# An eight-layer recurrent block with routed experts: the row of ones from the relu, the last norms reordered, 18 constant products in the head

## The chip, the cores and the metric

The kernel runs on one core of one Trainium2 chip, in one launch. The metric is the device time in microseconds of one execution; lower is better. Three executions of the kernel before gave 852.19 us in the median (851.09 to 852.88).

## The reference

The input x has 8 sequences of 512 rows of 128. It is normalised once (xn), and two branches read xn:

- Eight layers of linear attention and a feed-forward part: k and q go through elu + 1, `kv` is the sum over the sequence of k times v, `att = q kv z`, then `h = LN(h + att Wo + bo)` and `h = LN(h + gelu(h W1 + c1) W2 + c2)`, and a last norm. 
- One routed expert per sequence: the mean over the sequence of a normalised xn, a softmax over 8 experts, the largest taken, and with that expert's weights

```python
h = jax.nn.relu(jnp.einsum('bsd,bdh->bsh', z, W_down[idx]) + b_down[idx][:, None, :])
y = jnp.einsum('bsh,bhd->bsd', h, W_up[idx]) + b_up[idx][:, None, :]
return y * gate[:, None, None]
```

The output is `x + s * silu(expert branch)`, with s the first branch.

## The kernel before, in words

A unit is one sequence in one layer: 64 units. Work is staged as a software pipeline over 66 periods, each of about 12.7 us; in period p the attention of unit p, the first norm of unit p - 1, the feed-forward of unit p - 2 and the second norm of unit p - 3 run on the engines beside the projection of k and q for unit p + 1 and the transposes of the state of unit p + 2. The order on each engine is written by hand: `pe_period`, `act_period`, `dve_period` and `pool_period` give one period's instructions for TensorE, ScalarE, VectorE and GpSimd, and semaphores tie them together. Products are in f32; the k, q and up projections are split into a high and a low part (three products each), and an f32 product of TensorE leaves two records in the profile.

**The head.** SyncE and ScalarE issue the first loads. GpSimd makes the constants (ident, mean_f32, ones, centre, and later a memset of the last partition of `e_hid`, 1x4096, L1448), each counted in `const_ready`; it also forms the residual rows and the first `res_att` (L1051, L1054). VectorE takes statistics (L372, L376) and normalises the first two sequences. TensorE folds the first layer's weights (`pe_fold_att_first`, L238 and L241), transposes the first state (`pe_state_transpose`, L668), projects k and q (`pe_kq`, L680 to L682), turns the vector rows (`pe_cols`), and makes the first state product (`pe_kz`, L690). In period 0 VectorE copies g_sb (L1125), lays out the layers' vectors (`dve_cols`) and in `dve_affines` copies 4 columns (L194) and forms two matrices (L196, L198), before the shift of the third sequence and `dve_q_ks` (L1144); statistics of two more sequences follow in the same period.

**The experts.** After the routing in the last layer SyncE loads each sequence's expert: W_down (128x64), b_down, W_up with b_up as a 65th row. `pe_expert_down` (L592) multiplies into 64 partitions, `act_expert_relu` (L597) writes 64 partitions of `e_hid`, whose 65th partition holds the ones that GpSimd's memset wrote, and `pe_expert_up` (L610) contracts over 65 partitions, so that the row of ones brings in b_up.

**The last layer.** A finished sequence w gets a second norm and then the final one. In the periods 61 and 62 ScalarE normalises z_tm (`act_norm2`, L920) and directly behind it the final norm of sequences 0 and 1 (`act_final_norm`, L928), both at the period's end, ahead of the next period's gelu. `dve_den`/`dve_rden` (L1158) are in every period. Behind the last period the order is written out: TensorE does up, down, the transposes of z1 (L727) and expert products; VectorE does `dve_h2_tail` (L1205), statistics of seven slots (`dve_tail_stats`, L1241, L1245; they fill `tl_mv`), `dve_tail_shift` (L1249, L1251) and for sequences 6 and 7 `dve_last_affine` (gain step L1213, scale step L1218) in PSUM; ScalarE does the last rstd's (`act_tail_rstd`, L941, L943), and the silus (L630) after one more table load; GpSimd multiplies and adds (L1284, L1289) and the sequences go out.

Of the kernel before, what the change touches and what calls it, by code (L numbers as in the profile page):

```python
# [6 lines left out]
P = 128  # L7
# [4 lines left out]
def build(nc, x, Wq, bq, Wk, bk, Wv, bv, Wo, bo, g1, be1, g2, be2, W1, c1, W2, c2, gf, bef,  # L12
# [23 lines left out]
    with ExitStack() as ctx:  # L36
# [197 lines left out]

        def pe_fold_att_first(pe):
            pe.wait_ge(s["const_ready"], CONSTS_EARLY)
            pe.wait_ge(s["raw_a0"], 3 * 16)
            nc.tensor.matmul(up_ps[1][:, 0:3 * D], centre[:, :], raw_att[:, :, :].rearrange("p a d -> p (a d)"),  # L238
                             start=True, stop=False)
            pe.wait_ge(s["raw_b0"], 3 * 16)  # L240
            nc.tensor.matmul(up_ps[1][:, 0:3 * D], mean_f32[0:1, :], b_row[0:1, 0:3 * D],  # L241
                             start=False, stop=True).then_inc(s["xa_ps"], 1)
# [80 lines left out]
        ew_down = sb("ew_down", [P, SEQS, HID])  # L323
        eb_down = sb("eb_down", [HID, SEQS])
# [33 lines left out]
        CONSTS, CONSTS_EARLY = 12, 6  # L358
# [213 lines left out]
        def pe_expert_down(pe, i):  # L572
# [19 lines left out]
            nc.tensor.matmul(e_down_bank[i][0:HID, :], ew_down[:, w, :], zf_fm[:, w, :], start=True, stop=True).then_inc(s["e_down"], 1)  # L592

        def act_expert_relu(act, i):
            w = EXPERTS[i]
            act.wait_ge(s["e_down"], i + 1)
            nc.scalar.activation(e_hid[0:HID, i, :], e_down_bank[i][0:HID, :], ACT.Relu,  # L597
                                 bias=eb_down[:, w:w + 1]).then_inc(s["e_hid_s"], 1)

        def pe_expert_up(pe, i):  # L600
            w = EXPERTS[i]
            pe.wait_ge(s["e_hid_s"], i + 1)
            if i == 0:
                pe.wait_ge(s["const_ready"], CONSTS)
            elif i == 1:
                pe.wait_ge(s["h1_s"], UNITS)
# [318 lines left out]
        def act_final_norm(act, w):  # L925
            for t in range(TT):
# [32 lines left out]
        def act_period(act, l, b, between=None, behind_keys=None):  # L959
# [15 lines left out]
            if proj:  # L975
                act_q_exp(act, p + 1)
            if p == UNITS - 1:
                act_expert_relu(act, 0)
                act_norm2(act, p, (b - 3) % SEQS)
# [10 lines left out]
            if fin and p < UNITS - 1:  # L990
                act_final_norm(act, p - 5 - FIRST_LAST)
# [216 lines left out]
        def dve_last_affine(dve, w, slot):  # L1208
            bank = tail_ps[w]
            dve.wait_ge(s["tl_mv_s"], TT * (slot + 1))  # L1210
            for t in range(TT):
                i = slot * TT + t
                nc.vector.scalar_tensor_tensor(bank[:, t, :], bank[:, t, :], tl_mv[:, i, 0:1], fin_bc[:, 0, :],  # L1213
                                               ALU.subtract, ALU.mult).then_inc(s["last_c"], 1)
            dve.wait_ge(s["last_c"], TT * (w - 5))
# [31 lines left out]
        def dve_tail_shift(dve, first, last, calls):  # L1247
# [3 lines left out]
            nc.vector.tensor_scalar(tl_sh[:, c], tl_m[:, c], -1.0, 1.0, ALU.mult, ALU.add).then_inc(s["tl_sh_s"], 1)  # L1251
# [109 lines left out]
        with nc.Block() as block:  # L1361
            @block.sync
            def _(sp):
# [40 lines left out]
                for b in range(SEQS):  # L1404
                    e = sp.value_load(expert_i[b:b + 1, 0:1], min_val=0, max_val=E - 1)
                    sp.dma_start(ew_down[:, b, :], W_down[bass.ds(e, 1)].rearrange("a d h -> d (a h)")).then_inc(expert_in[b], 16)
                    sp.dma_start(eb_down[:, b:b + 1], b_down[bass.ds(e, 1)].rearrange("a h -> h a")).then_inc(expert_in[b], 16)
# [9 lines left out]
            def _(pool):  # L1417
# [30 lines left out]
                nc.gpsimd.memset(e_hid[HID:HID + 1, :, :], 1.0).then_inc(c, 1)  # L1448
                pool.wait_ge(c, 11)
                nc.gpsimd.iota(expert_m8[:, :], pattern=[[1, E]], base=-E, channel_multiplier=0,  # L1450
# [26 lines left out]
            def _(pe):  # L1477
                pe_fold_att_first(pe)
                pe_state_transpose(pe, 0, 0)
                pe.wait_ge(s["qk_ready"], 2)  # L1480
                pe_period(pe, -1, SEQS - 1)
                pe_cols(pe)
                pe_period(pe, 0, 0, lambda: pe_fold_w1_first(pe))
# [11 lines left out]
                pe_down(pe, last - 1, range(TT))  # L1495
                pe_z1_transpose(pe, last, UNITS)
                pe_expert_up(pe, 1)
# [69 lines left out]
            def _(dve):  # L1567
# [58 lines left out]
                dve_expert_gate(dve, 1)  # L1626
                dve_h2_tail(dve, last)
# [5 lines left out]
                dve_last_affine(dve, 6, S_W6)  # L1633
                dve.wait_ge(s["tl_r_s"], 2)
                dve_tail_shift(dve, S_F5, S_F5, 2)
                dve_last_affine(dve, 7, S_W7)
# [33 lines left out]
```

## Time and profile before

| what | value |
|---|---|
| median of three executions | 852.19 us (851.09 to 852.88) |
| the profiled execution's own time | 852.55 us |
| its span | 850.8 us |
| TensorE busy | 806.7 us, 95% of the span |
| VectorE busy | 764.9 us, 90% |
| ScalarE busy | 735.8 us, 86% |
| GpSimd busy | 415.2 us, 49% |

The profile is of one execution. A row of the timeline gives start, duration, engine, line and operation, and in brackets how long the engine was idle before it and what ended that. Transposes and matmuls of one group stand in one row with xN records. A busy TensorE is not TensorE at its peak: its records overlap, and their length depends on the granted clock.

### The profile page before, as it was taken

Reading aid. Unit: us, or ns where it says so; the run is one execution under the profiler, and the core shown is the slowest. Engines: PE = TensorE matmul, PEld = TensorE weight load, DVE = VectorE, ACT = ScalarE, POOL = GpSimd, SP = SyncE. Lnnn points to the kernel's source line nnn. Section 1 sums busy time; section 2 is a strip of 40 time slices with the busy share of each in tenths; the row PEclk is TensorE's granted clock in tenths of the full one; section 3 lists DMA queues with packets and bytes.
Section 4 is the critical chain, followed back from the end, with each engine's and each line's share of the span. In section 5 each row is a group of like instructions: output and inputs, shape, how many; then the busy total and the mean of one; then the engine's idle time right before and its main releaser. Section 6 shows DMA issues by size and latency. Waiting matters only on the chain.

```text
span 850.8 us, 19233 instructions
## 1 busy us (share of the span) xinstructions
PE 806.7 (95%) x5914; PEld 734.9 (86%) x5914; DVE 764.9 (90%) x2670; ACT 735.8 (86%) x1315; POOL 415.2 (49%) x395
## 2 busy tenths in 40 slices
PE   5698999999999999999999999999999999999993
PEld 3588899989999999999999999999999998988862
DVE  5888998999999898999899898998999898999877
ACT  2479999988999899988999899998999899989875
POOL 5243444454544454544454444444454454456667
PEclk9789999999999999999999999999999999999996
DMA  5300200101010100101010000101000000000002
GB/s 149 90 2 1 45 1 2 35 2 44 2 35 2 45 2 1 35 2 45 1 27 11 25 20 2 35 2 45 1 21 16 1 2 2 1 20 8 1 14 87
DMA packets 26264, 18.76 MB, mean 22 GB/s; under 512 B 4354, under 2 KB 22195, under 8 KB 26164
## 3 DMA queue, kind: packets, MB, share of 16 engines
q1 hardware_dynamic: 25300, 16.95, 7.2%
q8 instruction: 49, 0.80, 0.4%
q10 hardware_dynamic: 864, 0.59, 0.2%
q14 instruction: 51, 0.42, 0.2%
HBM read 15.43 MB, written 2.10 MB: 21 GB/s over the span
## 4 chain that ended last, share of the span: by engine, by line
PE 80%; DVE 9%; ACT 6%; issue 3%; POOL 1%; DMA 0%; POOLq 0%; ACTq 0%; DVEq 0%
PE down_ps L759 21%; PE att_ps L720 7%; PE small_ps L690 6%; PE up_ps L749 5%; PE up_ps L751 5%; PE up_ps L750 5%; PE t_ps L668 5%; PE t_ps L727 4%; PE kq_ps L680 3%; PE kq_ps L681 3%; PE kq_ps L682 3%; DVE z_lo L1044 3%; ACT z_hi L914 2%; PE up_ps L711 2%; PE small_ps L698 2%
## 5 line engine op out<-in xcount | busy, mean ns | idle before, releaser
L759 PE MATMUL down_ps<-w_use,hid 128*128 128x128 f32 x2048 | 259.5, 275 | 0.7 <-ACT hid L865 0.7
L759 PEld LDWEIGHTS down_ps<-w_use,hid 128*128 128x128 f32 x2048 | 243.8, 192 | 2.7 <-ACT hid L865 2.7
L1062 POOL TENSOR_TENSOR res_ffn<-z_tm,g_ffn 128x512 f32<-128x512 f32 x64 | 81.9, 1279 | 241.2 <-DVE k_e L1175 235.9
L1051 POOL TENSOR_TENSOR res_att<-z_tm,g_att 128x512 f32<-128x512 f32 x64 | 82.5, 1288 | 155.1 <-DVE h L1002 155.1
L865 ACT ACTIVATE hid<-up_ps 128x512 f32<-128x512 f32 x192 | 113.4, 592 | 22.2 <-PE up_ps L751 14.7
L1014 DVE BATCH_NORM_STATS2 st<-h 128x6 f32<-128x128 f32 x504 | 107.5, 276 | 0.1
L920 ACT ACTIVATE z_tm<-h,shift,rstd 128x128 f32<-128x128 f32 x248 | 101.5, 482 | 1.3 <-DVE shift L1031 1.3
L749 PE MATMUL up_ps<-z_hi,w_hi 128*128 128x512 f32 x192 | 86.4, 450 | 2.2 <-ACT hid L865 1.7
L1065 POOL TENSOR_TENSOR res_ffn<-res_ffn,ffn_row 128x512 f32<-128x512 f32 x64 | 84.0, 1313 | 5.0
L1054 POOL TENSOR_TENSOR res_att<-res_att,att_row 128x512 f32<-128x512 f32 x64 | 82.3, 1286 | 5.0
L680 PE MATMUL kq_ps<-w_kq_hi,zq_hi 128*128 128x256 f32 x256 | 82.0, 320 | 1.5 <-DVE zq_lo L957 1.5
L985 ACT ACT_TABLE_LOAD x63 | 80.8, 1283 | 1.1
L966 ACT ACT_TABLE_LOAD x62 | 79.5, 1283 | 1.1
L751 PE MATMUL up_ps<-z_lo,w_hi 128*128 128x512 f32 x192 | 75.6, 394 | 0.0
L750 PE MATMUL up_ps<-z_hi,w_lo 128*128 128x512 f32 x192 | 75.3, 392 | 0.0
L690 PEld LDWEIGHTS small_ps<-k_phi,z_tm 128*128 128x128 f32 x512 | 68.1, 194 | 7.5 <-DVE k_phi L1182 2.1
L1039 DVE TENSOR_SCALAR z_tm<-h,rstd,shift 128x128 f32<-128x128 f32 x256 | 71.5, 343 | 2.3
L681 PE MATMUL kq_ps<-w_kq_lo,zq_hi 128*128 128x256 f32 x256 | 73.2, 286 | 0.0
L682 PE MATMUL kq_ps<-w_kq_hi,zq_lo 128*128 128x256 f32 x256 | 72.8, 285 | 0.0
L1044 DVE TENSOR_TENSOR z_lo<-t_ps,z_hi 128x512 fp32r<-128x512 f32 x64 | 44.3, 692 | 31.6 <-ACT z_hi L914 31.6
L690 PE MATMUL small_ps<-k_phi,z_tm 128*128 128x128 f32 x512 | 68.6, 277 | 2.0 <-DVE k_phi L1182 2.0
L720 PE MATMUL att_ps<-kvo,q_n 128*128 128x128 f32 x512 | 69.6, 280 | 0.0
(223 smaller groups left out, 1966.4 us busy)
## 6 DMA issues: line engine op xcount, KB each, us to landing
raw_w<-in_L_attn_W SPq DMA_DIRECT2D x15, 256.0 KB, 4.6
out_y<-gate_tm SPq DMA_DIRECT2D x8, 256.0 KB, 2.2
bias_bc<-in_L_attn_c SPq DMA_DIRECT2D x7, 256.0 KB, 4.8
x_tm<-in_L_attn_x SPq DMA_DIRECT2D x3, 512.0 KB, 7.8
raw_rows<-in_L_attn_be SPq DMA_DIRECT2D x15, 64.0 KB, 4.3
raw_g<-in_L_attn_g SPq DMA_DIRECT2D x14, 64.0 KB, 3.2
x_tm<-in_L_attn_x SPq DMA_DIRECT2D x2, 256.0 KB, 3.5
raw_rows<-in_L_attn_bo SPq DMA_DIRECT2D x8, 64.0 KB, 3.9
```

The costliest lines, as they stand in the source:

```text
L680: nc.tensor.matmul(to, tile(zq_hi, t), w_kq_hi[:, :], start=True, stop=False)
L681: nc.tensor.matmul(to, tile(zq_hi, t), w_kq_lo[:, :], start=False, stop=False)
L682: last = nc.tensor.matmul(to, tile(zq_lo, t), w_kq_hi[:, :], start=False, stop=True)
L690: last = nc.tensor.matmul(G_PS, z_tm[:, b, t, :], k_phi[:, t, :], start=(t == 0), stop=(t == TT - 1))
L720: last = nc.tensor.matmul(att_ps[:, t, :], tile(q_n, t), kvo[:, :], start=True, stop=True)
L749: nc.tensor.matmul(up_bank[j], w_hi, z1_hi[:, :], start=True, stop=False)
L750: nc.tensor.matmul(up_bank[j], w_lo, z1_hi[:, :], start=False, stop=False)
L751: nc.tensor.matmul(up_bank[j], w_hi, z1_lo[:, :], start=False, stop=True).then_inc(s["up"], 1)
L759: last = nc.tensor.matmul(down_ps[:, t, :], hid[:, j, t * P:(t + 1) * P], w2_use[:, j, :], start=(j == 0), stop=(j == FC - 1))
L865: nc.scalar.activation(hid[:, j, :], up_bank[j], ACT.Gelu).then_inc(s["gelu"], 1)
L920: nc.scalar.activation(z_tm[:, b, t, :], h2[:, b % 2, t, :], ACT.Identity, scale=rstd[:, i:i + 1], bias=shift[:, i:i + 1]).then_inc(s["z2n ...
L1014: nc.vector.bn_stats(st[:, first + t, :], h[:, t, :]).then_inc(s[st_s], 1)
```

## The change

Seven edits, in the order of the diff:

1. `pe_keep_busy` issues products of two constants, ident and centre, into `att_ps`, which nothing has used yet: 8 ahead of the fold of the first weights, 4 behind the transposes of the first state, 6 behind `pe_cols`.
2. `ew_down` gets a 65th column of zeros for each sequence and `eb_down` a 65th partition of ones, both by small memsets on GpSimd, in place of the memset of `e_hid`; the product goes into 65 partitions and the relu of 0 + 1 writes the ones. `const_ready` counts one more, and the wait for it moves from `pe_expert_up(0)` to `pe_expert_down(0)` and the first relu.
3. `act_final_norm` is called for two tiles behind q_exp, and for two at the period's end.
4. `dve_last_affine` becomes `dve_last_gain` and `dve_last_scale`, and the gain steps stand earlier in VectorE's order.
5. `tl_sh` is computed by a subtraction of two tensors instead of a tensor_scalar.
6. For the last unit but one the last tile of down stands behind the transposes of z1.
7. The two loads into the enlarged tiles write the first 64 columns and partitions.

```diff
@@ -232,8 +232,14 @@
+        def pe_keep_busy(pe, products):
+            for _ in range(products):
+                nc.tensor.matmul(att_ps[:, 0, :], ident[:, :], centre[:, :], start=True, stop=True)
         def pe_fold_att_first(pe):
             pe.wait_ge(s["const_ready"], CONSTS_EARLY)
+            pe_keep_busy(pe, 8)
             pe.wait_ge(s["raw_a0"], 3 * 16)
             nc.tensor.matmul(up_ps[1][:, 0:3 * D], centre[:, :], raw_att[:, :, :].rearrange("p a d -> p (a d)"),
                              start=True, stop=False)
@@ -320,8 +326,9 @@
         wr_sb = sb("wr_sb", [P, E])
         br_bc = sb("br_bc", [SEQS, E])
         expert_i = sb("expert_i", [SEQS, 1], I32)
-        ew_down = sb("ew_down", [P, SEQS, HID])
-        eb_down = sb("eb_down", [HID, SEQS])
+        ew_down = sb("ew_down", [P, SEQS, HID + 1])
+        eb_down = sb("eb_down", [HID + 1, SEQS])
         ew_up = sb("ew_up", [HID + 1, SEQS, D])
         e_hid = sb("e_hid", [HID + 1, SEQS, S])
         st_x = sb("st_x", [P, SEQS * TT, 6])
@@ -355,7 +362,7 @@
         tl_r = sb("tl_r", [P, 7 * TT])
         tl_m = sb("tl_m", [P, 7 * TT])
         tl_sh = sb("tl_sh", [P, 7 * TT])
-        CONSTS, CONSTS_EARLY = 12, 6
+        CONSTS, CONSTS_EARLY = 13, 6
@@ -589,20 +596,22 @@
                 pe.wait_ge(s["z1lo_s"], UNITS)
             elif i == 7:
                 pe.wait_ge(s["gelu"], (UNITS - 1) * FC + 3)
-            nc.tensor.matmul(e_down_bank[i][0:HID, :], ew_down[:, w, :], zf_fm[:, w, :], start=True, stop=True).then_inc(s["e_down"], 1)
+            if i == 0:
+                pe.wait_ge(s["const_ready"], CONSTS)
+            nc.tensor.matmul(e_down_bank[i][0:HID + 1, :], ew_down[:, w, :], zf_fm[:, w, :], start=True, stop=True).then_inc(s["e_down"], 1)
         def act_expert_relu(act, i):
             w = EXPERTS[i]
             act.wait_ge(s["e_down"], i + 1)
-            nc.scalar.activation(e_hid[0:HID, i, :], e_down_bank[i][0:HID, :], ACT.Relu,
+            if i == 0:
+                act.wait_ge(s["const_ready"], CONSTS)
+            nc.scalar.activation(e_hid[:, i, :], e_down_bank[i][0:HID + 1, :], ACT.Relu,
                                  bias=eb_down[:, w:w + 1]).then_inc(s["e_hid_s"], 1)
         def pe_expert_up(pe, i):
             w = EXPERTS[i]
             pe.wait_ge(s["e_hid_s"], i + 1)
-            if i == 0:
-                pe.wait_ge(s["const_ready"], CONSTS)
-            elif i == 1:
+            if i == 1:
                 pe.wait_ge(s["h1_s"], UNITS)
             if i < TANH:
                 pe.wait_ge(s["ew_scaled"], i + 1)
@@ -922,8 +931,9 @@
-        def act_final_norm(act, w):
-            for t in range(TT):
+        def act_final_norm(act, p, w, tiles):
+            act.wait_ge(s["shift_s"], p)
+            for t in tiles:
                 i = 2 * TT + t
                 nc.scalar.activation(z_tm[:, w, t, :], z_tm[:, w, t, :], ACT.Identity, scale=rstd[:, i:i + 1],
                                      bias=shift[:, i:i + 1]).then_inc(s["zf_n"], 1)
@@ -974,6 +984,8 @@
                 behind_keys()
             if proj:
                 act_q_exp(act, p + 1)
+            if fin and p < UNITS - 1:
+                act_final_norm(act, p, p - 5 - FIRST_LAST, (0, 1))
             if p == UNITS - 1:
                 act_expert_relu(act, 0)
                 act_norm2(act, p, (b - 3) % SEQS)
@@ -988,7 +1000,7 @@
             if ln2 and p < UNITS - 1:
                 act_norm2(act, p, (b - 3) % SEQS)
             if fin and p < UNITS - 1:
-                act_final_norm(act, p - 5 - FIRST_LAST)
+                act_final_norm(act, p, p - 5 - FIRST_LAST, (2, 3))
             if between:
                 between()
@@ -1205,13 +1217,16 @@
             nc.vector.tensor_tensor(tail_ps[u - FIRST_LAST][:, :, :], down_ps[:, :, :], res_ffn[:, u % 2, :, :],
                                     ALU.add).then_inc(s["h2_s"], 1)
-        def dve_last_affine(dve, w, slot):
+        def dve_last_gain(dve, w, slot):
             bank = tail_ps[w]
             dve.wait_ge(s["tl_mv_s"], TT * (slot + 1))
             for t in range(TT):
                 i = slot * TT + t
                 nc.vector.scalar_tensor_tensor(bank[:, t, :], bank[:, t, :], tl_mv[:, i, 0:1], fin_bc[:, 0, :],
                                                ALU.subtract, ALU.mult).then_inc(s["last_c"], 1)
+        def dve_last_scale(dve, w, slot):
+            bank = tail_ps[w]
             dve.wait_ge(s["last_c"], TT * (w - 5))
             for t in range(TT):
                 i = slot * TT + t
@@ -1248,7 +1263,7 @@
             c = slice(first * TT, last * TT + TT)
             nc.vector.tensor_tensor(tl_m[:, c], tl_mv[:, c, 0], tl_r[:, c], ALU.mult).then_inc(s["tl_mr_s"], 1)
             dve.wait_ge(s["tl_mr_s"], calls)
-            nc.vector.tensor_scalar(tl_sh[:, c], tl_m[:, c], -1.0, 1.0, ALU.mult, ALU.add).then_inc(s["tl_sh_s"], 1)
+            nc.vector.tensor_tensor(tl_sh[:, c], ones[:, c], tl_m[:, c], ALU.subtract).then_inc(s["tl_sh_s"], 1)
         def dve_final_norm(dve, w):
             dve.wait_ge(s["shift_s"], UNITS - 1)
@@ -1403,8 +1418,8 @@
                 sp.wait_ge(s["routed"], 1)
                 for b in range(SEQS):
                     e = sp.value_load(expert_i[b:b + 1, 0:1], min_val=0, max_val=E - 1)
-                    sp.dma_start(ew_down[:, b, :], W_down[bass.ds(e, 1)].rearrange("a d h -> d (a h)")).then_inc(expert_in[b], 16)
-                    sp.dma_start(eb_down[:, b:b + 1], b_down[bass.ds(e, 1)].rearrange("a h -> h a")).then_inc(expert_in[b], 16)
+                    sp.dma_start(ew_down[:, b, 0:HID], W_down[bass.ds(e, 1)].rearrange("a d h -> d (a h)")).then_inc(expert_in[b], 16)
+                    sp.dma_start(eb_down[0:HID, b:b + 1], b_down[bass.ds(e, 1)].rearrange("a h -> h a")).then_inc(expert_in[b], 16)
                     sp.dma_start(ew_up[0:HID, b, :], W_up[bass.ds(e, 1)].rearrange("a h d -> h (a d)")).then_inc(expert_in[b], 16)
                     sp.dma_start(ew_up[HID:HID + 1, b, :], b_up[bass.ds(e, 1)]).then_inc(expert_in[b], 16)
@@ -1445,8 +1460,10 @@
                 pool_w2(pool, 0, False)
                 pool_period(pool, 0, 1)
                 pool.wait_ge(s["t2m"], 2)
-                nc.gpsimd.memset(e_hid[HID:HID + 1, :, :], 1.0).then_inc(c, 1)
+                nc.gpsimd.memset(eb_down[HID:HID + 1, :], 1.0).then_inc(c, 1)
                 pool.wait_ge(c, 11)
+                nc.gpsimd.memset(ew_down[:, :, HID:HID + 1], 0.0).then_inc(c, 1)
+                pool.wait_ge(c, 12)
                 nc.gpsimd.iota(expert_m8[:, :], pattern=[[1, E]], base=-E, channel_multiplier=0,
                                allow_small_or_imprecise_dtypes=True).then_inc(c, 1)
                 pool.wait_ge(c, CONSTS)
@@ -1477,9 +1494,11 @@
             def _(pe):
                 pe_fold_att_first(pe)
                 pe_state_transpose(pe, 0, 0)
+                pe_keep_busy(pe, 4)
                 pe.wait_ge(s["qk_ready"], 2)
                 pe_period(pe, -1, SEQS - 1)
                 pe_cols(pe)
+                pe_keep_busy(pe, 6)
                 pe_period(pe, 0, 0, lambda: pe_fold_w1_first(pe))
                 for b in range(1, SEQS):
                     pe_period(pe, 0, b)
@@ -1492,8 +1511,9 @@
                 last = UNITS - 1
                 pe_up(pe, last - 1, UNITS, range(FC))
                 pe_expert_down(pe, 1)
-                pe_down(pe, last - 1, range(TT))
+                pe_down(pe, last - 1, (0, 1, 2))
                 pe_z1_transpose(pe, last, UNITS)
+                pe_down(pe, last - 1, (3,))
                 pe_expert_up(pe, 1)
                 pe_up(pe, last, UNITS, range(FC))
                 pe_down(pe, last, range(TT))
@@ -1624,16 +1644,18 @@
                 dve_tail_stats(dve, S_F4, z_tm[:, 4], s["y_s"], 5)
                 dve_tail_stats(dve, S_W6, small_ps, s["h2_s"], p - 1)
                 dve_expert_gate(dve, 1)
+                dve_last_gain(dve, 6, S_W6)
                 dve_h2_tail(dve, last)
                 dve.wait_ge(s["tl_r_s"], 1)
                 dve_tail_shift(dve, S_F3, S_F4, 1)
                 dve_tail_stats(dve, S_W7, down_ps, s["h2_s"], p)
                 dve_tail_stats(dve, S_F5, z_tm[:, 5], s["y_s"], 6)
-                dve_last_affine(dve, 6, S_W6)
+                dve_last_scale(dve, 6, S_W6)
+                dve_last_gain(dve, 7, S_W7)
                 dve.wait_ge(s["tl_r_s"], 2)
                 dve_tail_shift(dve, S_F5, S_F5, 2)
-                dve_last_affine(dve, 7, S_W7)
+                dve_last_scale(dve, 7, S_W7)
                 dve_tail_stats(dve, S_F6, small_ps, s["y_d"], TT)
                 dve_tail_stats(dve, S_F7, down_ps, s["y_d"], 2 * TT)
```

## Rows read from the trace of the kernel before

**Rows 1.** The page: span, and the chain that ended last, by engine.

```profile
span 850.8 us, 19233 instructions
...
PE 80%; DVE 9%; ACT 6%; issue 3%; POOL 1%; DMA 0%; POOLq 0%; ACTq 0%; DVEq 0%
```

**Rows 2.** The chain of work from 0 to 60 us: start, us, what.

```profile
20.36 3.25 DVE lv L194
```

**Rows 3.** Timeline, GpSimd and VectorE, 18 to 24 us: start, us, engine, line, op.

```profile
18.73 1.26 POOL L1054 TENSOR_TENSOR res_att<-res_att,att_row 128x512 f32<-128x512 f32 x1
...
19.68 0.29 DVE L1125 COPY g_sb<-small_ps 128x128 f32<-128x128 f32 x1 [0.97 <-PE small_ps L690]
...
20.06 3.50 POOL L1448 MEMSET e_hid<- 1x4096 f32 x1
...
23.63 0.34 DVE L196 TENSOR_SCALAR aff_att<-centre,lv 128x128 f32<-128x128 f32 x1
```

**Rows 4.** All executions of line L194, durations in ns.

```profile
L194 DVE TENSOR_SCALAR lv<-layer_vecs x8: 152/154/3236, 20.4 to 657.7; 128x4 f32<-128x4 f32 x8
```

**Rows 5.** Timeline of the head: GpSimd's centre, then TensorE's products.

```profile
1.94 0.45 POOL L1427 TENSOR_TENSOR centre<-ident,mean_f 128x128 f32<-128x128 f32 x1
...
5.87 1.62 PE L238 MATMUL up_ps<-raw_att,centre 128*128 128x384 f32 x2 [5.87 <-DMA raw_att<-in_L_attn_Wv]
...
8.99 1.11 PE L668 MATMUL t_ps<-ident,z_tm 128*128 128x128 f32 x4
...
12.17 0.41 PE L682 MATMUL kq_ps<-w_kq_hi,zq_lo 128*128 128x256 f32 x1
...
12.38 0.41 PE L680 MATMUL kq_ps<-w_kq_hi,zq_hi 128*128 128x256 f32 x1
...
17.57 2.07 PE L690 MATMUL small_ps<-k_phi,z_tm 128*128 128x128 f32 x8 [1.97 <-DVE k_phi L1182]
...
23.45 0.28 PE L682 MATMUL kq_ps<-w_kq_hi,zq_lo 128*128 128x256 f32 x1
```

**Rows 6.** Tile x_tm from 5.7 to 6.2 us: its loads' landing; then VectorE's timeline.

```profile
DMA to landing us min/median/max: 6.9/7.4/7.8
...
13.21 0.86 DVE L372 BATCH_NORM_STATS2 st_x<-x_tm 128x6 f32<-128x128 f32 x4
```

**Rows 7.** Timeline of periods 62 and 63, by engine.

```profile
791.15 0.60 ACT L914 ACTIVATE z_hi<-t_ps 128x512 fp32r<-128x512 f32 x1 [0.98 <-PE t_ps L727]
...
795.22 1.64 ACT L928 ACTIVATE z_tm<-z_tm,shift,rstd 128x128 f32<-128x128 f32 x4
...
797.39 0.50 PE L749 MATMUL up_ps<-z_hi,w_hi 128*128 128x512 f32 x1 [0.86 <-ACT hid L865]
...
800.57 1.27 POOL L1268 TENSOR_TENSOR z_tm<-z_tm,fin_bc 128x512 f32<-128x512 f32 x1
...
800.76 1.13 DVE L1158 TENSOR_SCALAR den_e<-den 128x64 f32<-128x64 f32 x1
```

**Rows 8.** Timeline of the tail, 816 to 840 us, by engine.

```profile
816.53 0.50 PE L749 MATMUL up_ps<-z_hi,w_hi 128*128 128x512 f32 x1 [0.52 <-DVE z_lo L1044]
...
824.10 0.70 DVE L1205 TENSOR_TENSOR down_ps<-down_ps,res_ffn 128x512 f32<-128x512 f32 x1 [2.72 <-PE down_ps L759]
...
824.93 1.19 DVE L1251 TENSOR_SCALAR tl_sh<-tl_m 128x8 f32<-128x8 f32 x1
...
828.64 1.10 DVE L1213 SCALAR_TENSOR_TENSOR small_ps<-small_ps,tl_mv,fin_bc 128x128 f32<-128x128 f32 x4
...
830.82 0.43 DVE L1249 TENSOR_TENSOR tl_m<-tl_mv,tl_r 128x4 f32<-128x4 f32 x1
...
836.57 0.30 ACT L941 ACTIVATE tl_ln<-tl_mv,eps_col 128x8 f32<-128x8 f32 x1 [1.34 <-DVE tl_mv L1245]
...
839.19 1.27 POOL L1284 TENSOR_TENSOR gate_tm<-gate_tm,z_tm 128x512 f32<-128x512 f32 x1 [1.48 <-ACT gate_tm L630]
```

**Rows 9.** Windows: us, busy time of each engine (records), granted clock (PEclk), DMA.

```profile
29.60:33.50 3.90, 3.87 (x17) 3.63 (x18) 2.49 (x5) 1.59 (x4) 0.00 (x0) 0.50 0.37 71
```

## The prediction

> **What bounds the kernel now.** I read the page first. TensorE carries 80% of the chain that ended last [rows 1]. So in the 60-odd middle periods, whose code the change leaves alone, nothing is to be had. The change touches the first 25 us, where TensorE waits for data and for small VectorE steps, and the last 75 us, where the expert part and the norms hang on VectorE and ScalarE. I therefore read the chain at the start. One step there is out of scale: VectorE's L194, 3.25 us for a copy of 4 numbers per partition [rows 2]. The timeline of the two engines around it shows why: GpSimd's memset of e_hid runs from 20.06 for 3.50, to 23.56, L194 starts inside it, and its successor L196 starts at 23.63 [rows 3]. The same line takes 0.154 us in the median of its 8 executions [rows 4]. VectorE was held until GpSimd let go.
>
> **Part 1, the row of ones out of the relu.** Taken away: one memset of 1x4096 on GpSimd, 3.50 us. Added: a memset of 1x8, one of 128x8 with a wait more, one column in each of 8 expert weights and one partition in each of 8 relus; the moving 512 columns of a product stay 512. No row shows memsets of that form: the bounds are nothing, and 0.3 us for both on VectorE's path if they hold it as the long one did; I take 0.15. What L194 gives back is 3.25 - 0.15 = 3.1 us [rows 2, 4], all of it on the path: L196, L198, the shift of x and the first q_ks L1144 stand behind it on VectorE. That is the gain if nothing else moved.
>
> **Part 2, the 18 products.** Two records each, 36 records on TensorE. The matmuls of the head run at the low level, 1.2 GHz: a record of kq takes 0.41 us at 12.17 and the next starts 0.21 later; at 23.45, the last of its kind before the first q_ks, it takes 0.28 [rows 5]. (The column of the granted clock shows no low value so early; I go by the durations.) L690's eight records of 128 columns f32 take 2.07 with their tail, so about 0.21 to 0.24 each at the low level, and I take 0.21, the step of kq's, and half of it at the high level. 16 records are 3.4 us. The first eight products start when centre is there, near 2.4, and end near 5.8; L238 starts at 5.87, when its weights have landed [rows 5]. They cost nothing, but with no margin: up to 0.2 us if they start late. The next four (8 records, 1.7 us low, 0.9 high) stand between the transposes, which end at 10.1, and L680 at 11.61, which waits for VectorE's zq_lo; cost 0 to 0.2. The last six (12 records, 2.6 low, 1.4 high) begin near 15.6 and must be through when k_phi is, 17.57: at the low level they are 0.6 us late, at the high level not at all.
>
> What they can give: TensorE would be continuously busy from 2.4 on instead of from 5.87. In the kernel before its records became short only at 23.45, after it had worked through kv and kq(1); 4 us of work from 5.87 to 10.1, a third of it with a single row of weights, did not do it [rows 5]. With 7 us on end I take the high level as reached before kq(0), with 4 chances in 5. Then kq(0), 12 records at 0.21 us, saves 1.2 to 1.4 us, the transposes and L690 1.0 more [rows 5]. Little of that arrives. First, stats of the third sequence need x_tm, issued at 5.74 with 6.9 us to landing, so 12.6, against 13.21 now: VectorE's aggregate ends at most 0.6 earlier, and ScalarE's rstd stands before q_exp in its order [rows 6]. So k_phi gains about 1.6 us, and g_sb, 19.68 now, comes near 17.3. Second, and this decides, GpSimd's pair on res_att holds VectorE then: its second half L1054 runs 18.73 to 19.99 [rows 3], its start is set by GpSimd's own order and by landings that the change leaves alone. L194 and the two L196, L198 behind it are of the kind that was held. I expect L196 at about 20.05 instead of 23.63: 3.6 us for parts 1 and 2 together, less the 0.15 for the small memsets, so **3.4 us**, 0.3 more than part 1 alone. Behind it VectorE is busy without a gap up to q_nt, so this arrives.
>
> The Trainium skill, TensorE: Matmul & The Clock Gate, What's actually happening, says the array's default is the throttled clock and activity releases it. By that rule all of kq(0), L690 and kq(1) run at 2.4 GHz, and by their rows the clock alone would be worth some 3.6 us; the trace agrees as far as 23.45, where records got short after work. What it leaves to the end is the business of rival D.
>
> **Part 3, act_final_norm in two halves (periods 61 and 62).** ScalarE idles 0.98 us before z1_hi L914 at 791.15; two of the four tiles of L928 (half of 1.64) fit in. What is left before gelu is 0.8 us shorter, and TensorE's idle before L749 at 797.39, 0.86 us, which ScalarE's hid ends, closes by that much [rows 7]. Twice, so at most 1.6. VectorE takes part back: den_e L1158 at 800.76 is held for 1.13 us by GpSimd's L1268 of 800.57 [rows 7], and where VectorE arrives earlier it meets GpSimd's operation before that. Bounds 0 and 1.6; I take **1.0**.
>
> **Part 4, z1 transposes before the last tile of down.** They free z1_hi and z1_lo earlier by up to a tile of down. TensorE then has that tile and expert_up(1) to do before it can start up; the gain can't exceed the 0.52 us that it idles before L749 at 816.53 [rows 8]. Bounds 0 and 0.52; **0.3**.
>
> **Part 5, last_affine split.** VectorE idles 2.72 us before L1205 at 824.10; the gain step of sequence 6 (L1213, 1.10 us at 828.64) goes in there. What then ends earlier is tl_mv of the last slot, for which ScalarE's L941 waits (836.57, idle 1.34), then the table load, the first silu and GpSimd's L1284 at 839.19, idle 1.48 [rows 8]. All three idle times exceed 1.1. **1.1**. The gain step of sequence 7 only swaps with a wait that is over by then: 0.
>
> **Part 6, tl_sh by tensor_tensor.** tl_sh L1251 takes 1.19 us at 824.93, held by GpSimd. But tl_m L1249, a tensor_tensor out of SBUF, takes 0.43 us at 830.82 as well [rows 8]: this form is held too. So 0; bounds: a gain of 1.0 if it were not, a loss of 1.2 if the second shift, which now slips through, is caught.
>
> By the Trainium skill, SBUF — State Buffer, SBUF: two separate sides, a VectorE operation with two SBUF inputs is locked out by a GpSimd operation that reads SBUF. The trace agrees, with the 0.43 us; this speaks against part 6.
>
> **The sum.** 3.4 + 1.0 + 0.3 + 1.1 = 5.8 us off the profiled execution, whose own time was 852.55 (span 850.8 [rows 1] and 1.75 around it). The median shown, 852.19, lies 0.36 lower; I subtract from it: **846.4 us**.
>
> **Rivals.** (B) The clock stays low through the head. The last six products then delay L690 by 0.6, and part 1 gives 3.1 - 0.6 = 2.5: total 4.9, 847.3. For it: 4 us of work near 6 us did not lift the clock. 0.15. (C) The tail gives back: VectorE, arriving earlier, is caught by one more GpSimd operation (1.26 us each) at the second tl_sh or at den_e. Part 5 or 3 is lost, total about 3.9: 848.3. For it: L1158 and L1251 are both caught now. 0.18. (D) VectorE's L194 and L196 slip between GpSimd's two halves. Then the 2.4 us by which g_sb is earlier arrive too: 3.1 + 2.4 + 2.4 = 7.9, 844.3. 0.12. (E) Slower: the new start puts VectorE's den_e behind GpSimd's res_att in many middle periods, as at 800.76, about 1.0 us each. It decides from 6 periods on; in 12 it would be +12 - 5.8, 858.4. Against it: in a period both engines are tied to each other by waits, not to the start. 0.03. (F) The head's gain is absorbed in layer 0 by an engine I took for idle and the tail gives 1 us at most: 851.2. 0.04. The forecast keeps 0.48.
>
> **Range and chances.** A measurement of this kernel tells about 0.2% (1.7 us) from no change. (B), (C) and (D) lie within 844.3 and 848.3; also the granted clock is 0.50 from 29.6 to 33.5 in the kernel before [rows 9], and where it falls may move: 0.5 us on each side. 843.8 to 848.8. Faster 0.93, within 0.2% 0.04, slower 0.03.
>
> **What would show it.** Of each step: L194 at 0.15 us or ended by GpSimd's res_att, L196 near 20; L681 and L690 short in the head; L928 in two rows, and no idle time over 0.3 before L749 after them; L941 of the last slots 1.1 us closer to the last L1205; tl_sh as long as a GpSimd operation lets it be. I am wrong if q_ks L1144 of the first unit starts later than 21.5, if the stretch from the first q_ks to period 60 changes by over 1 us, or if the last L1205 to the end stays as long as it was.

## The result, and the profile after

The changed kernel takes 845.05 us in the median of 4 executions (843.67 to 845.28), the kernel before 852.01 us of 4: a ratio of 0.9915, 95% interval 0.9898 to 0.9932, or 7.0 us less. The forecast was 5.8 us less and 846.4 us, in a range of 843.8 to 848.8. The profiled execution took 845.23 us with a span of 843.5, so 7.3 us of span less than in the profile before.

The page of the changed kernel, span and chain, against [rows 1]:

```profile
span 843.5 us, 19308 instructions
...
PE 79%; DVE 10%; ACT 6%; issue 3%; POOL 1%; DMA 0%; POOLq 0%; DVEq 0%; ACTq 0%
```

The head, in its timeline (start, duration, engine, line; lines are up to 22 further down than before: L1137 copies g_sb, L1156 is q_ks, L1066 the second half of GpSimd's res_att):

```profile
2.45 3.42 PE L238 MATMUL att_ps<-centre,ident 128*128 128x128 f32 x16 [2.45 <-POOL centre L1442]
...
5.71 0.81 PE L244 MATMUL up_ps<-raw_att,centre 128*128 128x384 f32 x2
...
9.64 0.46 POOL L279 TENSOR_TENSOR row_sum<-raw_rows 128x128 f32<-128x128 f32 x1 [6.02 <-DMA raw_rows<-in_L_attn_c]
...
16.20 1.16 PE L699 MATMUL small_ps<-k_phi,z_tm 128*128 128x128 f32 x8 [0.80 <-DVE k_phi L1194]
...
17.03 1.27 POOL L1066 TENSOR_TENSOR res_att<-res_att,att_row 128x512 f32<-128x512 f32 x1
17.40 0.29 DVE L1137 COPY g_sb<-small_ps 128x128 f32<-128x128 f32 x1
...
18.07 0.26 DVE L194 TENSOR_SCALAR lv<-layer_vecs 128x4 f32<-128x4 f32 x1
...
18.36 0.10 POOL L1463 MEMSET eb_down<- 1x8 f32 x1
...
18.36 0.35 DVE L196 TENSOR_SCALAR aff_att<-centre,lv 128x128 f32<-128x128 f32 x1
...
19.15 0.69 DVE L1156 SCALAR_TENSOR_TENSOR q_ks<-q_elu,small_ps 128x512 f32<-128x512 f32 x1
```

The eight products take 3.42 us and end at 5.87, and the fold behind them is short at once: 0.81 us for what took 1.62 [rows 5]. L194 takes 0.26 us in place of 3.24. L196 starts at 18.36 in place of 23.63 [rows 3]. The first q_ks is 5.3 us earlier.

But then some of it goes again. VectorE between the first and the second q_ks, and TensorE in the same stretch (L729 is the attention product, L699 the state product):

```profile
24.36 0.66 PE L720 MATMUL up_ps<-ident,q_nt 128*128 128x128 f32 x4 [2.10 <-DVE q_nt L1181]
...
25.70 1.99 PE L729 MATMUL att_ps<-kvo,q_n 128*128 128x128 f32 x8 [0.25 <-ACT q_n L916]
27.48 1.90 PE L699 MATMUL small_ps<-k_phi,z_tm 128*128 128x128 f32 x8
```

```profile
30.41 0.84 DVE L395 TENSOR_TENSOR mr_x<-mv_x,r_x 128x8 f32<-128x8 f32 x1
31.29 0.17 DVE L397 TENSOR_SCALAR shift_x<-mr_x 128x8 f32<-128x8 f32 x1
31.39 0.69 DVE L1156 SCALAR_TENSOR_TENSOR q_ks<-q_elu,small_ps 128x512 f32<-128x512 f32 x1
```

TensorE idles 2.10 us ahead of L720, and the records behind it are long again. The state product takes 1.90 us, nearly the 2.07 of 17.57 before [rows 5], and not 1.16 as at 16.20. The second q_ks is 4.47 us earlier than before (31.39 against 35.86 in the timeline before), and from there to q_ks of unit 61 the distance stays between 4.38 and 4.55 us. The middle periods gave nothing and took nothing: 723.5 us before and 723.6 after from the second q_ks to that of unit 60, about 12.3 us a period.

The tail, ScalarE, VectorE and GpSimd, against [rows 7, 8] (L938 is the final norm, L1037 m_r, L1225 the gain step, L1217 the last h2, L1266 tl_sh, L951 the last rstd, L1299 GpSimd's gate):

```profile
771.78 0.86 ACT L938 ACTIVATE z_tm<-z_tm,shift,rstd 128x128 f32<-128x128 f32 x2
773.26 0.60 ACT L923 ACTIVATE z_hi<-t_ps 128x512 fp32r<-128x512 f32 x1 [0.61 <-PE t_ps L736]
...
777.80 0.87 ACT L938 ACTIVATE z_tm<-z_tm,shift,rstd 128x128 f32<-128x128 f32 x2
...
829.26 0.30 ACT L951 ACTIVATE tl_ln<-tl_mv,eps_col 128x8 f32<-128x8 f32 x1 [0.17 <-DVE tl_mv L1260]
```

```profile
783.28 0.68 DVE L1037 TENSOR_TENSOR m_r<-mv,rstd 128x12 f32<-128x12 f32 x1
...
815.14 1.13 DVE L1225 SCALAR_TENSOR_TENSOR small_ps<-small_ps,tl_mv,fin_bc 128x128 f32<-128x128 f32 x4
817.94 0.70 DVE L1217 TENSOR_TENSOR down_ps<-down_ps,res_ffn 128x512 f32<-128x512 f32 x1 [1.67 <-PE down_ps L768]
...
818.78 1.19 DVE L1266 TENSOR_TENSOR tl_sh<-ones,tl_m 128x8 f32<-128x8 f32 x1
```

```profile
831.88 1.27 POOL L1299 TENSOR_TENSOR gate_tm<-gate_tm,z_tm 128x512 f32<-128x512 f32 x1 [0.31 <-ACT gate_tm L639]
```

The final norm stands in two rows of two tiles. The gain step fills the wait ahead of the last h2, whose idle time shrinks from 2.72 to 1.67 us. The last rstd comes 11.32 us after the last h2 in place of 12.47. tl_sh takes 1.19 us as a tensor_tensor, exactly what it took as a tensor_scalar [rows 8].

The tail's length, from q_ks of unit 60 to the end, is 91.42 us before and 88.54 after. In three profiles of the changed kernel it is 88.54 to 88.61, in four of kernels with the old tail 91.29 to 91.49. The tail repeats to 0.2 us and can be read from one profile; the head can't, as the runs show.

### The profile page after: what moved, and what is told of

It is laid out like the page before. It is cut to its first block, busy times and chain, and to the rows that moved or that the text cites. A ratio compares the mean times of both kernels' runs of the same rounds, so it can differ in the third digit from the quotient of the medians.

```text
span 843.5 us, 19308 instructions
## 1 busy us (share of the span) xinstructions
PE 806.4 (96%) x5950; PEld 736.7 (87%) x5950; DVE 763.7 (91%) x2670; ACT 735.8 (87%) x1315; POOL 412.1 (49%) x396
## 4 chain that ended last, share of the span: by engine, by line
PE 79%; DVE 10%; ACT 6%; issue 3%; POOL 1%; DMA 0%; POOLq 0%; DVEq 0%; ACTq 0%
PE down_ps L768 21%; PE att_ps L729 6%; PE small_ps L699 6%; PE up_ps L758 5%; PE up_ps L760 5%; PE up_ps L759 5%; PE t_ps L677 4%; PE t_ps L736 4%; PE kq_ps L689 3%; PE kq_ps L690 3%; PE kq_ps L691 3%; DVE z_lo L1056 3%; ACT z_hi L923 2%; PE up_ps L720 2%; PE small_ps L707 2%
## 5 line engine op out<-in xcount | busy, mean ns | idle before, releaser
L1066 POOL TENSOR_TENSOR res_att<-res_att,att_row 128x512 f32<-128x512 f32 x64 | 82.3, 1287 | 5.0
L699 PEld LDWEIGHTS small_ps<-k_phi,z_tm 128*128 128x128 f32 x512 | 67.8, 193 | 6.4 <-DVE k_phi L1194 1.0
L729 PE MATMUL att_ps<-kvo,q_n 128*128 128x128 f32 x512 | 69.5, 280 | 0.2 <-ACT q_n L916 0.2
L699 PE MATMUL small_ps<-k_phi,z_tm 128*128 128x128 f32 x512 | 68.3, 277 | 0.8 <-DVE k_phi L1194 0.8
```

Of the source, the lines that this page charges most:

```text
L699: last = nc.tensor.matmul(G_PS, z_tm[:, b, t, :], k_phi[:, t, :], start=(t == 0), stop=(t == TT - 1))
L729: last = nc.tensor.matmul(att_ps[:, t, :], tile(q_n, t), kvo[:, :], start=True, stop=True)
```

## The experiments

The runs were made in three batches of four, the first two on chip 7 and the last on chip 1. Each ratio is to executions of the kernel before in the same batch, with its 95% interval. Differences said to be by the ratios are taken from these and not from the medians; the two disagree by up to 0.7 us.

**The row of ones alone.** The kernel before with

```diff
-                nc.gpsimd.memset(e_hid[HID:HID + 1, :, :], 1.0).then_inc(c, 1)
+                nc.gpsimd.memset(eb_down[HID:HID + 1, :], 1.0).then_inc(c, 1)
                 pool.wait_ge(c, 11)
+                nc.gpsimd.memset(ew_down[:, :, HID:HID + 1], 0.0).then_inc(c, 1)
+                pool.wait_ge(c, 12)
```

and what belongs to it. 

> The kernel before with the row of ones out of the relu alone (no products, tail as before). My theory: L194 of the first unit falls from 3.24 us to under 0.3 us, nothing else in the head changes, the first q_ks starts near 21.3 instead of 24.42, and the time is 3.1 us below the kernel before. Rival (the memset only stood in front of GpSimd's other work): L194 is held by another operation of GpSimd and the gain is under 2 us.

Measured: 846.88 us against 851.61, ratio 0.9953 (0.9936 to 0.9969), 4.0 us less by the ratio and 4.7 by the medians. L194 is short:

```profile
18.67 0.17 DVE L194 TENSOR_SCALAR lv<-layer_vecs 128x4 f32<-128x4 f32 x1
18.87 0.35 DVE L196 TENSOR_SCALAR aff_att<-centre,lv 128x128 f32<-128x128 f32 x1
```

The first q_ks starts at 19.67, not 21.3. The landings at the start were 0.8 us earlier in this execution, and the state product already ran at the high level, so g_sb was at 18.00 in place of 19.68. And behind q_nt the attention product is short too:

```profile
24.88 0.66 PE L719 MATMUL up_ps<-ident,q_nt 128*128 128x128 f32 x4 [0.61 <-DVE q_nt L1178]
...
26.46 1.16 PE L728 MATMUL att_ps<-kvo,q_n 128*128 128x128 f32 x8 [0.48 <-ACT q_n L915]
```

The first q_ks is 4.75 us earlier than before: 3.07 by L194 and 1.68 by g_sb. The measured 4.0 us fit the 3.1 of L194 and about one more, but the interval (2.6 to 5.5 us) holds 3.1 alone too. TensorE idles only 0.61 us ahead of L719, where it idled 2.7 us with the memset.

**The 18 products alone.** The kernel before with the three calls of `pe_keep_busy`. 

> The kernel before with the 18 products alone (the memset of e_hid stays). My theory: TensorE is at the high level from about 6 us, g_sb comes near 17.4, but L196 runs into the 3.5 us memset, which begins behind res_att near 18.3 to 20, so q_ks starts near 22 to 23.5 and the time is 1 to 2 us below the kernel before: the two parts are not additive, their sum needs both. Rival (the products are worth their full 2.3 us at g_sb whatever GpSimd does): 2.3 us or more below. Second rival (the clock is not theirs to lift): no change.

Measured: 851.44 us of 12 executions against 851.61, ratio 1.0001 (0.9989 to 1.0012). The second rival's number, but not its reason, for the clock did rise: the fold behind the products is at the high level (0.88 us) and g_sb comes at 16.47. It is VectorE that meets the memset, two lines further on, at L198:

```profile
17.35 1.37 DVE L196 TENSOR_SCALAR aff_att<-centre,lv 128x128 f32<-128x128 f32 x1
18.64 3.64 DVE L198 TENSOR_SCALAR aff_ffn<-centre,lv 128x128 f32<-128x128 f32 x1
18.90 3.39 DVE L394 TENSOR_TENSOR mr_x<-mv_x,r_x 128x4 f32<-128x4 f32 x1
...
22.43 0.69 DVE L1150 SCALAR_TENSOR_TENSOR q_ks<-q_elu,small_ps 128x512 f32<-128x512 f32 x1
```

```profile
18.70 3.50 POOL L1454 MEMSET e_hid<- 1x4096 f32 x1
```

3.2 us won up to g_sb, 2.0 left at q_ks, and 0.6 at the second q_ks (35.23 against 35.86).

**The head alone.** The changed kernel with `act_final_norm` and `dve_last_affine` in one piece, the last tile of down ahead of the transposes, and tl_sh by tensor_scalar. 

> The changed kernel with its tail put back (final norm in one piece, last affine in one piece, last tile of down ahead of the transposes, tl_sh by tensor_scalar). My theory: 4.5 us below the kernel before, with q_ks of unit 0 5.3 us earlier and of unit 1 on 4.5 us earlier, unchanged to the end. Rival (an earlier load of this one execution made the head look better): 3.4 us or less below.

Measured: 848.35 us of 11 executions against 851.61, ratio 0.9963 (0.9949 to 0.9976), 3.2 us less. The rival is right: the head with both parts is worth no more than the row of ones alone, whose ratio was 0.9953 (the intervals overlap). The profiled execution was the longest of the 11, at 850.93, with q_ks of unit 60 only 1.48 us earlier than before: one profile of the head is one draw. In it VectorE's normalisation of z_tm took 3.26 us from 11.80 on, in place of 1.34 before, and g_sb came at 19.67, as late as before.

**Without products.** The changed kernel with the three calls taken out. 

> The changed kernel without its 18 products. My theory: 3.1 us of the head and 2.8 us of the tail remain, so 5.9 us below the kernel before and 1.1 to 1.4 us above the changed kernel. Rival (the products are worth nothing at the end, GpSimd bounds the head): within 0.4 us of the changed kernel's 7.0 us gain.

Measured: 844.43 us against 851.61, ratio 0.9921 (0.9906 to 0.9937), 6.7 us less by the ratio. My theory, 1.1 to 1.4 us above the changed kernel, missed, and the rival is right again: the products are worth nothing that shows here.

**The changed kernel again.** 

> The changed kernel itself, once more, as the yardstick on this chip and for a second profile. My theory now: the 18 products are worth nothing that can be measured, the rest is the row of ones and the tail; 6.5 to 7.2 us below the kernel before, and the tail in the profile is the same to 0.1 us, while the head differs by up to 1.5 us with the landing of the third residual row (9.6 to 11.4 us so far) and with where the granted clock falls. Rival (the first profile is typical to the last 0.1 us): the first q_ks again at 19.15 and the second at 31.39.

Measured: 845.69 us against 852.13, ratio 0.9922 (0.9909 to 0.9934), 6.4 us less. The first q_ks at 19.70, the second at 32.49, where the first profile had 19.15 and 31.39.

**The final norm back in one piece.**

```diff
-            if fin and p < UNITS - 1:
-                act_final_norm(act, p, p - 5 - FIRST_LAST, (0, 1))
...
-                act_final_norm(act, p, p - 5 - FIRST_LAST, (2, 3))
+                act_final_norm(act, p, p - 5 - FIRST_LAST, range(TT))
```

> The changed kernel with act_final_norm in one piece again. My theory: 1.4 us slower than the changed kernel (0.75 in period 61 and 0.66 in period 62, by the steps of q_ks), with TensorE idle 0.8 us before up again. Rival (GpSimd gives it back): under 0.5 us slower.

Measured: ratio 0.9935 (0.9921 to 0.9950), 1.1 us above the changed kernel by the ratios, whose intervals overlap; the trace decides. TensorE's idle time ahead of up is there again:

```profile
779.12 0.50 PE L758 MATMUL up_ps<-z_hi,w_hi 128*128 128x512 f32 x1 [0.82 <-ACT hid L874]
...
792.08 0.51 PE L758 MATMUL up_ps<-z_hi,w_hi 128*128 128x512 f32 x1 [0.86 <-ACT hid L874]
```

From q_ks of unit 60 to the end it takes 89.82 us against 88.54: this part is worth 1.28 us. By q_ks of unit 63 it was 1.4; 0.17 is given back where the z1 transposes of the last unit wait.

**The gain steps back.** `dve_last_gain` of sequences 6 and 7 directly ahead of their scale steps, as before. 

> The changed kernel with the gain step of sequences 6 and 7 back behind the statistics. My theory: 1.1 to 1.2 us slower than the changed kernel, all of it between the last h2 and the last rstd of ScalarE. Rival (ScalarE's relus and norms bound that stretch anyway): under 0.4 us slower.

Measured: ratio 0.9937 (0.9922 to 0.9951), 1.3 us above the changed kernel by the ratios, whose intervals overlap here too. The last h2 waits 2.72 us, the last rstd comes 12.48 us behind it and not 11.31, and ScalarE waits for it as before:

```profile
831.00 0.30 ACT L951 ACTIVATE tl_ln<-tl_mv,eps_col 128x8 f32<-128x8 f32 x1 [1.34 <-DVE tl_mv L1260]
```

**tl_sh on ScalarE, and GpSimd's first gate early.** The changed kernel with

```diff
-            nc.vector.tensor_tensor(tl_sh[:, c], ones[:, c], tl_m[:, c], ALU.subtract).then_inc(s["tl_sh_s"], 1)
...
+        def act_tail_shift(act, first, last, calls):
+            c = slice(first * TT, last * TT + TT)
+            act.wait_ge(s["tl_mr_s"], calls)
+            nc.scalar.activation(tl_sh[:, c], tl_m[:, c], ACT.Identity, scale=-1.0, bias=ones[:, 0:1]).then_inc(s["tl_sh_s"], 1)
...
+                final_gate(nc.gpsimd, pool, 0)
+                final_residual(nc.gpsimd, pool, 0)
                 pool_last_affine(pool, 5)
```

> A version meant to beat both: the changed kernel with tl_sh computed by ScalarE (an activation with scale -1 and bias 1) in place of VectorE, so that GpSimd can't hold it, and GpSimd's gate and residual of sequence 0 moved ahead of its last affine of sequence 5, into its idle 2.6 us. My theory (VectorE's held 1.19 us is on the path, GpSimd is then the next bound): 0.8 to 1.1 us faster than the changed kernel. Rival (GpSimd's last three pairs and VectorE's last seven operations end the kernel at their own pace): 0.3 us or less.

Measured: 844.74 us, ratio 0.9908 (0.9893 to 0.9923), 1.2 us below the changed kernel by the ratios. The tail is 87.40 us long against 88.61. The run made both edits, so their shares are not shown. The shift takes 0.29 us, with no hold by GpSimd:

```profile
821.14 0.29 ACT L944 ACTIVATE tl_sh<-tl_m,ones 128x8 f32<-128x8 f32 x1
...
829.88 0.29 ACT L956 ACTIVATE tl_ln<-tl_mv,eps_col 128x8 f32<-128x8 f32 x1
```

ScalarE is now busy from 823.17 up to this rstd, so its relus and norms seem to bound the stretch.

**Three more on one chip, to settle the products.** The changed kernel a third time: 

> The changed kernel once more, beside the two below on the same chip. My theory: 6 to 7.2 us below the kernel before. In its profile the stretch from the first to the second q_ks of the kernel takes 11.2 to 12.8 us, as in the five profiles with products so far, by where the granted clock lies at its low level between 20 and 32 us. Rival (products make no difference to that stretch): 10.1 to 10.4 us as in the two profiles without them that have the row of ones from the relu.

Without the products: 

> The changed kernel without its 18 products, once more. My theory: the time is that of the changed kernel within 0.7 us; what the products win up to g_sb (0.5 us or so) is lost between the first and the second q_ks, where the clock then falls at a worse place. Rival (they win at least the 1.2 us that the shorter head products promised): 1.2 us slower or more. Opposite rival (they cost): 1 us faster or more.

The better tail without the products: 

> The version with tl_sh on ScalarE and GpSimd's first gate early, and without the 18 products. My theory: 1.1 us below the changed kernel without products, within 0.7 us of the same version with products (8 us below the kernel before). Rival (the products matter in this version): more than 1 us apart from it.

Measured: 845.88 us (ratio 0.9924, 0.9911 to 0.9937), 845.03 us (0.9915, 0.9902 to 0.9928) and 844.09 us (0.9910, 0.9895 to 0.9924), against 852.53. With and without the products the intervals overlap each time; the point values of this pair even speak 0.8 us against them. The changed kernel's own stretch was 11.19 us this time.

**Products in the waits of the periods 0 and 1 as well.** The better tail, the 18 products, and

```diff
+            if isinstance(p, int) and p == 1:
+                pe.wait_ge(s["h1_s"], 1)
+                pe_keep_busy(pe, 6)
             if att:
                 if b == 0:
                     pe.wait_ge(s["wo_ready"], l + 1)
                 pe_kvo(pe, p)
+            if isinstance(p, int) and p == 0:
+                pe_keep_busy(pe, 8)
+            if isinstance(p, int) and p == 1:
+                pe_keep_busy(pe, 12)
```

> The version with tl_sh on ScalarE and GpSimd's first gate early, with the 18 products and 26 more of them: 8 behind kvo in period 0, and 6 and 12 around kvo in period 1, where TensorE idles 2 and 5 us. My theory (the granted clock falls in the head because TensorE idles for some us in both periods, and the low stretches near 24 to 30 and 36 to 43 us cost up to 2 us each): the clock stays at its high level from about 6 us to the end of the work in most executions, and the time is 2 to 4 us below the changed kernel. Rival (the low stretches lie where VectorE and ScalarE bound, as in the first 20 us): within 0.7 us of the 1.1 us that the tail gives. Second rival (the products come too late out of the way): slower.

Measured: 841.26 us (840.99 to 842.21), ratio 0.9872 (0.9858 to 0.9886), 11 us below the kernel before, and by the ratios 3.1 us below the same tail with 18 products and 3.2 below it without any. My theory's 2 to 4 us below the changed kernel is passed: it is 4.6 in this batch. TensorE in this kernel:

```profile
22.25 1.95 PE L238 MATMUL att_ps<-centre,ident 128*128 128x128 f32 x16
24.49 0.66 PE L720 MATMUL up_ps<-ident,q_nt 128*128 128x128 f32 x4 [0.30 <-DVE q_nt L1193]
...
25.84 1.16 PE L729 MATMUL att_ps<-kvo,q_n 128*128 128x128 f32 x8 [0.25 <-ACT q_n L923]
26.83 1.06 PE L699 MATMUL small_ps<-k_phi,z_tm 128*128 128x128 f32 x8
...
31.80 2.84 PE L238 MATMUL att_ps<-centre,ident 128*128 128x128 f32 x24
34.53 0.66 PE L736 MATMUL t_ps<-ident,z_tm 128*128 128x128 f32 x4
```

and its windows (the column behind GpSimd's busy time is the granted clock), then the same two of the changed kernel:

```profile
26.00:32.00 6.00, 5.62 (x48) 5.43 (x49) 5.68 (x20) 2.25 (x8) 2.58 (x2) 1.00 0.54 158
...
36.00:42.00 6.00, 5.21 (x32) 4.36 (x32) 5.86 (x29) 4.25 (x7) 2.33 (x2) 1.00 0.08 17
```

```profile
26.00:32.00 6.00, 5.51 (x32) 5.02 (x31) 4.09 (x11) 0.53 (x3) 2.55 (x2) 0.73 0.57 181
...
36.00:42.00 6.00, 4.86 (x21) 4.46 (x22) 5.30 (x19) 3.81 (x6) 2.55 (x2) 0.51 0.00 1
```

The head of all the profiles, by group; the second and third columns are starts of q_ks, the last two the granted clock of two windows:

| kernels | first q_ks | first to second | 26 to 32 us | 36 to 42 us |
|---|---|---|---|---|
| before | 24.42 | 11.44 | 0.57 | 0.87 |
| memset of e_hid and 18 products | 22.43 | 12.80 | 0.50 | 0.86 |
| row of ones and 18 products, 7 profiles | 19.15 to 21.34 | 11.19 to 12.80 | 0.50 to 0.86 | 0.51 to 0.75 |
| row of ones, no products, 4 profiles | 19.67 to 20.61 | 10.05 to 10.48 | 1.00 | 0.50 to 0.72 |
| row of ones and 44 products | 19.29 | 10.05 | 1.00 | 1.00 |

In the means of these profiles the first q_ks is 0.4 us earlier with the 18 products (19.88 against 20.25), and the stretch behind it 2.0 us longer (12.19 against 10.22). The measured times show less of a loss: by the ratios the pairs with and without them lie between 0.5 us for the products and 0.9 against, all within the noise.

In the changed kernel's first profile TensorE is through with kvo early and idles 2.10 us ahead of q_nt, and its clock is low when the attention and state products come. In the kernels without products the same work, in part at the low level, lasts longer and the clock is high behind it. The length of that one wait does not settle the level by itself: it is 1.22 to 2.69 us in the eight profiles with 18 products and 0.43 to 1.28 in the four without, so the two groups touch. With the 26 further products it is 0.30.

Against the same tail without any products (best_no_products), the profile of the 44 products has the first q_ks 1.32 us earlier and the second again 1.32. From the second to the third it takes 13.95 us against 15.03, with the granted clock at 1.00 against 0.51 in the window from 36 to 42 us: another 1.1 us. The three places of the 26 products were filled together, in one profile and four executions; which of them is needed, and whether they would do without the first 18, no run shows.

## Why the prediction was right, point by point

**The chain and L194: right.** The step that carried the sum, 3.1 us for L194 off the path, came: 0.17 to 0.26 us in place of 3.24 in the first two profiles without the memset, and 4.0 us (2.6 to 5.5) for that part alone. L194 was still held for up to 1.07 us by res_att in others, as the forecast allowed. What hangs on it was left out: with the stall gone and no products TensorE idles less ahead of q_nt, and its clock is high there.

**"Its start is set by GpSimd's own order and by landings that the change leaves alone": wrong as a number.** The order holds, the landing doesn't. GpSimd's first row sum started at 11.43 in the profile before and between 9.64 and 11.95 in the others, whatever the kernel; res_att's second half ended at 18.30 and not at 19.99, and L196 started at 18.36 and not near 20.05. The end of that half lay between 18.30 and 20.39 in the profiles after. So the bound that I put at 20 us moves by 2 us, and the 2.28 us by which g_sb was earlier in the first profile (17.40, forecast 17.3) did arrive beside the 2.98 of L194: together the 5.3 us at the first q_ks. That is the size of rival (D)'s head, but not its slip: L194 ended with the second half of res_att, and L196 came directly behind it, as in the main forecast. A slip between the halves is in the second profile of the changed kernel, where L194 ends at 17.84 and the second half starts at 17.89; L196 was held 1.37 us by it.

**The 18 products: 0.3 us forecast, nothing measured.** Size and sign are within the noise. The mechanism was half right: they start near 2.45, and kq(0) has short records, 0.28 us, in every profile that has them. They do not cost nothing, though. The fold behind the first eight starts at 5.71 to 6.03 with them and at 5.09 to 5.46 in the four profiles without, where its weights have landed; the prediction allowed 0.2 us. What cancels the rest was taken for a bound by GpSimd; against the kernels without products it is mainly TensorE's clock between 24 and 30 us. "Behind it VectorE is busy without a gap up to q_nt, so this arrives" was true as far as q_nt and silent on what comes next. Against the kernel before, whose clock was low there too, 0.8 us was lost between the two q_ks, 0.7 of it at mr_x (0.84 us), held by GpSimd's next res_att.

**The final norm: 1.0 forecast, 1.28 measured.** VectorE took back what was expected, m_r held for 0.68 and 0.70 us by GpSimd, and less of it.

**z1 transposes ahead of the last tile of down: 0.3 forecast, 0.44 left over** when 1.28 and 1.16 are taken from the tail's 2.88 us. In the trace the stretch from q_ks of unit 63 to the up behind these transposes is 17.70 us before and 17.41 after, and the 0.52 us of idle time ahead of up is gone. It was not undone by itself.

**The gain step: 1.1 forecast, 1.16 measured**, and no other engine came in the way: GpSimd's wait ahead of its last three gates shrank from 1.48 to 0.31 us.

**tl_sh by tensor_tensor: 0 forecast.** The row shows the same 1.19 us. It was not run by itself in its old form; on ScalarE it was worth 1.2 us together with GpSimd's early gate.

**The sum** 3.4 + 2.4 came as 4.4 + 2.9 in the profiled pair. By the medians of three measurements the change is worth 6.4 to 7.0 us, of which the tail is 2.9 and, as the products show nothing, the row of ones the rest.

Some luck is in the total. The first profile's head, 4.4 us, is a good draw: measured by itself the head was worth 3.2 us. And one of the prediction's own signs of being wrong was met in the changed kernel's second profile: the stretch from the first q_ks to that of unit 60 was to change by no more than 1 us, and it went from 734.96 us to 735.81, 736.59 and 734.55 in its three profiles.

## What to carry to other kernels

A VectorE step of a few numbers that takes microseconds was waiting for GpSimd here: look at what GpSimd runs at that moment, and shrink or move that, or give the step to ScalarE; the other form tried on VectorE waited as long. Products that are to keep TensorE's clock up need a look at the granted clock behind them: the 18 at the start alone gave nothing that could be measured, and with the waits of the next two periods filled as well the same kernel was 3.1 us faster. A gain in a head that depends on landings and on the clock needs several executions to be seen, one in the tail can be read off a single profile.

## What had not been expected

- With the memset and the products together two VectorE records lie under the memset (18.70 to 22.20): L198, a tensor_scalar, of 3.64 us in place of 0.34, and mr_x, a tensor_tensor of 128x4 out of SBUF, of 3.39 in place of 0.15. They end at 22.28 and 22.29. The prediction cited the Trainium skill, SBUF — State Buffer, SBUF: two separate sides, for a VectorE operation with two SBUF inputs being locked out by a GpSimd operation that reads SBUF. The memset reads nothing, but mr_x stood behind L198 in VectorE's order, so these rows do not show that the memset held mr_x itself, and they do not speak against the Trainium skill.
- All eight profiles of kernels with the 18 products and no further ones have the clock below its high level for part of 26 to 32 us, and none of the four with the row of ones and no products has; the kernel before reads 0.57. Where it falls within that stretch differs between executions of one kernel: three profiles of the changed kernel read 0.73, 0.63 and 0.86.
- The landing of three residual rows, with the same loads in front of it, moved by 2.3 us between the executions profiled, and by 1.0 us (9.64 to 10.68) among the three of the changed kernel.
